# First twelve score-maximum fills moved into the last five blocks of the projection stage, with its PSUM banks and input buffers laid out anew

## The reference

```python
mod = (silu(c) @ wmod).reshape(2, 6, 1, -1)
sa, ca, ga, sb, cb, gb = (mod[:, 0], ..., mod[:, 5])   # ga, gb are kept at least 0.25 from zero
h = layernorm(x) * (1 + ca) + sa
x = x + ga * attention(h)       # 16 heads of 16, causal, qkv = h @ W_qkv.T + b_qkv, then @ W_out.T + b_out
h = layernorm(x) * (1 + cb) + sb
x = x + gb * ffn(h)             # 256 -> 1024 -> 256, relu, each layer with 3 routed low-rank experts
```

## Time and profile before

| | us |
|---|---|
| median of 3 runs | 1308.25 (1307.49 to 1309.97) |
| profiled execution | 1304.39 |
| its span | 1302.4 |
| TensorE busy in the span | 1218.0 (94%) |
| VectorE busy | 933.2 (72%) |
| ScalarE busy | 800.5 (61%) |
| GpSimd busy | 178.0 (14%) |

### The profile page before, as it was taken

The page is one execution under the profiler, slowest core; times in us unless marked ns, Lnnn a source line. Parts: engine busy times, 40 slices in busy tenths (PEclk is TensorE's granted clock), DMA queues, the critical chain, the costliest instruction groups (busy, mean ns, idle before and its releaser), DMA issues.

```text
span 1302.4 us, 24602 instructions
## 1 busy us (share of the span) xinstructions
PE 1218.0 (94%) x9928; PEld 723.5 (56%) x9928; DVE 933.2 (72%) x1247; ACT 800.5 (61%) x1611; POOL 178.0 (14%) x153
## 2 busy tenths in 40 slices
PE   6988789999999999999999999999998899999997
PEld 5875334444444444444444444444444788898886
DVE  5877897888787887778887778786631576766553
ACT  4451466777777776767777667777675554444442
POOL 5205600000211000000000000200110132222310
PEclk9987798999999999999999999999899999999999
DMA  5793120031032021013003003500000222111100
GB/s 170 247 289 144 52 64 10 8 87 34 27 108 70 10 65 54 3 45 98 10 13 90 19 10 93 138 10 10 3 10 27 50 65 65 53 38 50 57 17 33
DMA packets 58121, 79.58 MB, mean 61 GB/s; under 512 B 12680, under 2 KB 28752, under 8 KB 58008
## 3 DMA queue, kind: packets, MB, share of 16 engines
q1 hardware_dynamic: 58008, 78.01, 20.3%
HBM read 47.57 MB, written 29.62 MB: 59 GB/s over the span
## 4 chain that ended last, share of the span: by engine, by line
PE 67%; DVE 12%; ACT 9%; issue 8%; SPq 2%; DMA 1%; POOL 0%; POOLq 0%; ACTq 0%; DVEq 0%
PE ps L907 21%; PE ps L882 17%; PE ps L863 9%; PE ps L391 8%; ACT prob L1121 7%; PE ps L1008 5%; DVE mx L1270 5%; PE ps L820 4%; PE ps L811 2%; DVE xhat L419 1%; DVE hid_lo L1413 1%; SPq L453 1%; ACT o_sb L1106 1%; DVE stats L409 1%; DMA wqkv_sb<-in_wqkvT 1%
## 5 line engine op out<-in xcount | busy, mean ns | idle before, releaser
L1121 ACT ACTIVATE prob<-ps 128x512 f32<-128x512 f32 (+3 forms) x1280 | 598.1, 537 | 263.0 <-PE ps L820 161.3
L1270 DVE TENSOR_REDUCE mx<-ps 128x2 f32<-128x1024 f32 (+1 forms) x512 | 594.0, 1188 | 148.2 <-PE ps L863 85.5
L882 PE MATMUL ps<-qst,kst 64*128 64x512 f32 (+3 forms) x1280 | 387.0, 446 | 18.9 <-ACT prob L1121 14.3
L882 PEld LDWEIGHTS ps<-qst,kst 64*128 64x128 f32 x1280 | 183.9, 188 | 270.2 <-ACT prob L1121 211.3
L907 PE MATMUL ps<-prob,vw 128*32 128x512 f32 (+3 forms) x3032 | 317.8, 492 | 3.4 <-ACT o_sb L1106 3.4
L863 PE MATMUL ps<-kst,qst 62*128 62x512 f32 (+3 forms) x1280 | 288.7, 425 | 21.5 <-DVE mx L1270 18.1
L863 PEld LDWEIGHTS ps<-kst,qst 62*128 62x128 f32 x1280 | 137.1, 193 | 95.4 <-DVE mx L1270 51.5
L907 PEld LDWEIGHTS ps<-prob,vw 128*32 128x32 f32 x3032 | 60.5, 108 | 86.9 <-issue 38.7
L820 PE MATMUL ps<-mask_kh,eye_h 64*128 64x128 bf16 x1024 | 99.6, 225 | 0.0
L1266 DVE TENSOR_REDUCE mx<-ps 128x4 f32<-128x512 f32 x64 | 60.9, 955 | 30.8 <-PE ps L811 30.4
L1413 DVE TENSOR_TENSOR hid_lo<-hidf,hid_hi 128x512 fp32r<-128x512 f32 x64 | 68.0, 1095 | 20.7 <-ACT hid_hi L1161 20.6
(11 more groups left out here) (157 smaller groups left out, 1350.5 us busy)
## 6 DMA issues: line engine op xcount, KB each, us to landing
qk_parts<-parts SPq DMA_DIRECT2D x32, 512.0 KB, 5.4
qst<-qk_parts SPq DMA_DIRECT2D x192, 64.0 KB, 2.4
kst<-qk_parts SPq DMA_DIRECT2D x192, 64.0 KB, 2.4
xs<-in_x SPq DMA_DIRECT2D x16, 512.0 KB, 8.4
o_all<-o_sb SPq DMA_DIRECT2D x32, 256.0 KB
o_raw<-o_all SPq DMA_DIRECT2D x16, 256.0 KB
rd<-rden_rows SPq DMA_DIRECT2D x16, 256.0 KB
out<-y SPq DMA_DIRECT2D x8, 512.0 KB, 3.2
```

The costliest lines, as they stand in the source:

```text
L882: last = pe.matmul(ps[:, L_BANK + (4 * n + h) % L_BUFS, 0:BLK - skip], kst[g % 2][rows, h // 2, t * P:(t + 1) * P], qst[g % 2][rows, h // ...
L1121: act.activation(prob[:, n % P_BUFS, h, 0:width], ps[:, L_BANK + i % L_BUFS, 0:width], ACT.Exp).then_inc(exp_done, 1)
L1270: dve.tensor_reduce(mx[:, u % 2, :, pairs[0], r, cb], ps[:, bank:bank + 2, 0:width], AX, ALU.max).then_inc(max_red, 1)
```

## The change

- **Fills.** Twelve fills (`EARLY`) run inside the first stage: two in block 3, three in blocks 4 and 5, two in blocks 6 and 7. Unit 0's turn becomes fill 7, right behind the first fill of unit 1, with negative, high and low directly ahead of it on VectorE. `ORDER[0]` is now these twelve, `ORDER[1]` holds 14 fills, and from `ORDER[2]` on nothing differs.
- **Banks.** Transposes use bank 0 alone (a half waits for the other's modulation), v banks 1 and 2, q/k products a ring of three, banks 3 to 5, early fills banks 6 and 7 alone, each waiting for the maximum of the one before.
- **x.** Five input buffers; blocks 2 to 5 are loaded ahead of the loop and in its first iteration.
- **Order.** TensorE: first half of `turn(n+1)`, product 0, second half, product 1, all fills of the block but the last two, product 2, one fill, product 3, one fill, v. VectorE: the maxima stand in like manner between the `qk_low` of single tiles. In block 0 the second half of the first transposes follows the second `columns`.
- **SyncE.** `store_m(0)` is issued ahead of block 6's `store_parts`.

The `maxima`, `negative` and like functions are moved ahead in the file unchanged, apart from taking the bank from `bank_of(e)`. The core of the diff:

```diff
+X_BUFS = 5
@@ max_events
-            if i - lag in ends:
+            if ends.get(i - lag, 0) > 0:
                 events.append((kind, ends[i - lag]))
+        if ends.get(i - 1) == 0:
+            events += [(kind, 0) for kind in ("neg", "high", "low", "turn")]
@@
+EARLY_OF = {3: 2, 4: 3, 5: 3, 6: 2, 7: 2}
+EARLY = sum(EARLY_OF.values())
+EARLY_FROM = {n: sum(c for m, c in EARLY_OF.items() if m < n) for n in EARLY_OF}
@@ slots
-    done = TURN_FILL[0] + 1 + 4
+    done = EARLY
@@ build_program
-        T_BANK, V_BANK, QK_BANK, COL_BANK = 0, 2, 4, 7
-        S_BANK, L_BANK, L_BUFS, O_BANK = 0, 4, 3, 7
+        V_BANK, QK_BANK, QK_BUFS, COL_BANK = 1, 3, 3, 7
+        T_BANK, S_BANK, L_BANK, L_BUFS, O_BANK = 0, 0, 4, 3, 7
+        def bank_of(e):
+            return 6 if e < EARLY else S_BANK + 2 * (e % 2)
+        def qk_bank(n, c):
+            return QK_BANK + (n * 2 * KC + c) % QK_BUFS
@@ SyncE
                 def load_x(n):
-                    until(sp, xhat_done, n - 1)
-                    sp.dma_start(xs[:, n % 2], xb_in[n]).then_inc(x_in[n % 2], 16)
+                    until(sp, xhat_done, n - X_BUFS + 1)
+                    sp.dma_start(xs[:, n % X_BUFS], xb_in[n]).then_inc(x_in[n % X_BUFS], 16)
-                load_x(2)
+                for n in range(2, X_BUFS):
+                    load_x(n)
                 for n in range(NBLK):
-                    if n + 3 < NBLK:
-                        load_x(n + 3)
+                    if n + X_BUFS < NBLK:
+                        load_x(n + X_BUFS)
+                    if n == NBLK - 2:
+                        store_m(0)
                     store_parts(n)
@@ TensorE
+                def turn(n, k):
                     pe.wait_ge(xhat_done, n + 1)
-                    until(pe, h_out, n * 2 * KC)
+                    until(pe, h_out, (n * KC + k) * 2)
...
+                def project_qk(n, c):
                     pe.wait_ge(h_lo, n + 1)
-                        until(pe, qk_lo, (n - 1) * 2 * KC + c + 1)
+                    until(pe, qk_lo, n * 2 * KC + c - QK_BUFS + 1)
...
                 def fill(e):
-                    until(pe, max_red, e - 1)
+                    until(pe, max_red, e if e < EARLY else e - 1)
...
+                columns(((0, 1), (1, 0)), COL_BANK)
+                pe.wait_ge(consts, 4)
+                turn(0, 0)
+                columns(((2, 4), (3, 3)), COL_BANK - 1)
+                turn(0, 1)
+                pe.wait_ge(w_lo, 2)
+                project_qk(0, 0)
+                project_qk(0, 1)
+                turn(1, 0)
+                project_qk(0, 2)
+                turn(1, 1)
+                project_qk(0, 3)
+                pe.wait_ge(setup, 2 * KC)
+                gate_rows()
+                project_v(0)
+                for n in range(1, NBLK):
+                    es = [EARLY_FROM[n] + k for k in range(EARLY_OF[n])] if n in EARLY_OF else []
+                    if n + 1 < NBLK:
+                        turn(n + 1, 0)
+                    project_qk(n, 0)
+                    if n + 1 < NBLK:
+                        turn(n + 1, 1)
+                    project_qk(n, 1)
+                    for e in es[:-2]:
+                        fill(e)
+                    project_qk(n, 2)
+                    for e in es[-2:-1]:
+                        fill(e)
+                    project_qk(n, 3)
+                    for e in es[-1:]:
+                        fill(e)
+                    project_v(n)
@@ VectorE, in the loop over blocks, after moments, rescale and low
-                    qk_low(n)
+                    qk_low(n, 0)
+                    qk_low(n, 1)
+                    for e in es[:-2]:
+                        events(e)
+                    qk_low(n, 2)
+                    for e in es[-2:-1]:
+                        events(e)
+                    qk_low(n, 3)
+                    for e in es[-1:]:
+                        events(e)
                     v_rows(n)
```

More of the change, by code:

```diff
@@ L162 @@
 SLOT_OF = {e: s for s, es in enumerate(ORDER) for e in es}
-STORE_M = {u: SLOT_OF[TURN_FILL[u]] for u in range(NU)}
+STORE_M = {u: SLOT_OF[TURN_FILL[u]] for u in range(1, NU)}
 STORE_O = {u: min(NS, LAST[u] + PV_LAG + 2) for u in range(NU)}
@@ L1208, in modulations, with qk_low @@
                                           1.0 - v % 2, None, ALU.add).then_inc(mod_out, 1)
[L1210 to L1215, removed]
+                def qk_low(n, c):
+                    dve.wait_ge(qk_hi, n * 2 * KC + c + 1)
+                    dve.scalar_tensor_tensor(out=parts[:, n % 2, 1, c, :], in0=ps[:, qk_bank(n, c), :],
+                                             scalar=bq_sb[:, c:c + 1], in1=parts[:, n % 2, 0, c, :].bitcast(F32),
+                                             op0=ALU.add, op1=ALU.subtract).then_inc(qk_lo, 1)
                 def v_rows(n):
@@ new lines, in invert, with low_o @@
+                def invert(g):
+                    for q in range(2):
+                        dve.wait_ge(o_stored[q], 16 * O_DMAS * NJ // 2 * (g + 1))
+                    until(dve, rden_stored[g % 2], 16 * (g // 2))
+                    dve.reciprocal(rden[:, g % 2, :], den[:, g % 2, :]).then_inc(rden_done, 1)
+                link = Links(dve, dve3)
+                def low_o(i):
+                    dve.wait_ge(o_hi, i + 1)
+                    dve.tensor_tensor(oT[1][:], o_raw[:, i % 2], oT[0][:].bitcast(F32), ALU.subtract).then_inc(o_lo, 1)
@@ new lines, in gated, with add_x @@
+                def gated(i, bank):
+                    q, b = i % 2, BLOCKS[i] // NJ
+                    return dve.tensor_tensor(x1[:, q], ps[:, bank:bank + 2, :].rearrange("p a (t d) -> p (a t) d", t=2),
+                                             gates[:, 0, b:b + 1, :].broadcast_to((P, TT, D)), ALU.mult)
+                def add_x(i):
+                    q = i % 2
+                    dve.wait_ge(xbias_done, i + 1)
+                    dve.tensor_tensor(x1[:, q], x1[:, q], xs2[:, q], ALU.add).then_inc(x1_done, 1)
+                    dve.wait_ge(x1_done, i + 1)
+                    statistics(dve, link, x1[:, q], stats2, mv2, var2)
@@ new lines, in front_modulate @@
+                def front_modulate(e):
+                    b = BLOCKS[0] // NJ
+                    dve.wait_ge(fill_done, e + 1)
+                    for k in range(KC):
+                        last = dve.tensor_scalar(hf2[:, k, :], ps[:, bank_of(e) + k, :],
+                                                 mod[:, b, 2, k:k + 1], mod[:, b, 3, k:k + 1], ALU.mult, ALU.add)
+                        if k < KC - 1:
+                            link(last, wait=False)
+                    last.then_inc(max_red, 1)
@@ new lines, in event @@
+                def event(i, ev):
+                    if ev[0] == "max":
+                        maxima(FILL_OF[i], ev)
+                    if ev[0] == "neg":
+                        negative(ev[1])
+                    if ev[0] == "high":
+                        m_high_part(ev[1])
+                    if ev[0] == "low":
+                        m_low_part(ev[1])
+                    if ev[0] == "turn":
+                        copy_turned(FILL_OF[i], ev[1])
+                    if ev[0] == "project":
+                        front_residual(FILL_OF[i])
+                    if ev[0] == "rescale":
+                        standardise_x1(0)
+                    if ev[0] == "turn_x":
+                        front_modulate(FILL_OF[i])
@@ L1223, in _, with events @@
+                def events(e):
+                    for i in range(FILLS[e - 1] + 1 if e > 0 else 0, FILLS[e] + 1):
+                        event(i, EVENTS[i])
                 dve.wait_ge(exp_c, 1)
@@ L1339, in front_modulate @@
-                def front_modulate(e):
-                    b = BLOCKS[0] // NJ
-                    dve.wait_ge(fill_done, e + 1)
-                    for k in range(KC):
-                        last = dve.tensor_scalar(hf2[:, k, :], ps[:, S_BANK + 2 * (e % 2) + k, :],
-                                                 mod[:, b, 2, k:k + 1], mod[:, b, 3, k:k + 1], ALU.mult, ALU.add)
-                        if k < KC - 1:
-                            link(last, wait=False)
-                    last.then_inc(max_red, 1)
@@ L1349, in _ @@
-                done = 0
-                for i, ev in enumerate(EVENTS):
-                    if ev[0] == "max":
-                        while INVERT[done] < SLOT_OF[FILL_OF[i]] - 1:
-                            invert(done)
-                            done += 1
-                        maxima(FILL_OF[i], ev)
-                    if ev[0] == "neg":
-                        negative(ev[1])
-                    if ev[0] == "high":
-                        m_high_part(ev[1])
-                    if ev[0] == "low":
-                        m_low_part(ev[1])
-                    if ev[0] == "turn":
-                        copy_turned(FILL_OF[i], ev[1])
-                    if ev[0] == "project":
-                        front_residual(FILL_OF[i])
```

(14 more changed lines are left out.)

187 lines of the change are left out of this document (73 added, 114 removed).

## The result

| | before | changed |
|---|---|---|
| median, us | 1307.87 (1306.21 to 1309.97, 4 runs) | 1332.35 (1329.35 to 1336.51, 4 runs) |
| profiled execution, us | 1304.39 | 1333.6 |
| its span, us | 1302.4 | 1331.7 |

The ratio is 1.0193, 95% interval 1.0172 to 1.0214. The forecast was 1330, slower.

The account below looks back on a forecast made before the run. It took TensorE, with three input waits, to bound the first stage, then VectorE's maxima; +11.0 + 5.3 + 13.0 - 12.3 = +17.0, +5.6 for the clock, made +22.6: about 1330 us, range 1318 to 1341.

Parts of the forecast that it names:

- The ring's wait and the two engines taking turns: First stage: each block's fourth q/k product waits for the first's low part on VectorE; TensorE stands 2.4 us.
- Block 0: First block: late first product and a wait before the fourth; block 1 starts at 45.9 instead of 34.90, +11.0 us.
- Blocks 1 and 2: First-stage blocks without fills: 12.0 us each, 2.7 more than before, together +5.3 us.
- Blocks 3 to 7: First-stage blocks with early fills: stalls at fills 3, 6 and the turn; 67.7 us against 54.7, +13.0.
- The clock: TensorE's pauses in the first stage: one fall in block 0, one more later, 2.8 us a fall, together +5.6.
- the third rival: First stage: the clock falls in every pausing block, +34 us, 1342; 20 in 100.
- Fill 12 after V: Start of attention: VectorE starts fill 12 2.9 us after the last V product instead of 15.2, saving 12.3 us.
- The sum: Whole kernel: +17.0 us at full clock, +5.6 for the clock, +22.6 in all; median about 1330.
- the shift reaches the end one for one: After step 0 the order of fills is unchanged, so a shift there was taken to reach the end in full.
- The faster rival: Fourth q/k product finds its bank free, blocks 1 and 2 stay at 9.34 us; about 1298; 8 in 100.

Follow-up runs that it names:

- late4: late3 with the q/k products going round a ring of four banks instead of three; 1304.19 us, ratio 0.9966.
- order: Changed kernel, only VectorE's and ScalarE's order altered: product 0's low part ahead of low(n+1) and standardising, its high part between modulations; 1306.91 us, ratio 1.0005.
- busy3: late3 with unread matmuls ahead of each block's fourth product, 8 a block and 32 in block 0; 1330.02 us, ratio 1.0179.
- after2: The changed kernel, unaltered, measured and profiled a second time; 1331.78 us, ratio 1.0192.
- late3: Changed kernel with the twelve early fills moved behind the first stage, in two pairs of banks, ring of three kept; 1336.59 us, ratio 1.0231.
- x5: The kernel before with five input buffers and nothing else; 1299.87 us, ratio 0.9953.
- b0: Changed kernel with one product, the fourth of block 0, put into the free bank 6; 1329.68 us, ratio 1.0179.
- tailb: x5b with unit 0's six fills inside blocks 6 and 7, in the transposes' first bank pair; 1300.11 us, ratio 0.9943.
- x5b: x5 with the 24 stack loads of blocks 2 and 3 issued behind the last stored parts; 1299.12 us, ratio 0.9934.

## Why the prediction was right, point by point

- **The ring's wait and the two engines taking turns.** Right, in mechanism and size. The low part of product 0 ends at 7.7 us into a block by the working; the fourth product started 8.09 us after the block's start in blocks 1 and 2 (56.58 - 48.49). late4 gives the ring its fourth bank back and the loss goes. order leaves it and takes away what stood ahead of the low part, and the loss goes too: the cause is the two together, as the step put it.
- **Block 0.** 20.4 expected for the first product, 20.86 found; 36.75 for the fourth, 36.50; 45.9 for block 1 at full clock, 48.49 found. The fall was counted, and at its 2.8 us it would be 48.7.
- **Blocks 1 and 2** at 12.0: 12.42 in the block without a fall, and 12.4 in busy3. 0.4 us of handoffs a block were missing.
- **Blocks 3 to 7.** 13.4, 14.8, 17.2, 11.8, 10.5 expected; 14.8, 16.6, 19.1, 12.1, 10.4 found. The stalls stand where they were put (fills 3 and 6, the turn). The sum was 67.7 and is 73.0; of the 5.3 that are missing 5.1 are in blocks 3 to 5, where the clock fell; three falls at busy3's price would be 4.65 (an estimate), the rest handoffs.
- **The clock was the mis-sized term.** I took two falls at 2.8 us. There were more, cheaper ones: of the five blocks with a pause only block 1 had none in the first profile and all five had one in the second (after2), as in late3. In after2 block 0 ends 1.3 us earlier instead (47.19 against 48.49), so how often and how long the clock is low differs between executions of one kernel. Price by busy3: 1.55 us. A fall here lasted about 3.3 us (an estimate: PEclk 0.88 over 13.94 us), where the row of before had 6.2 us at the lower level. Over block 0 and blocks 2 to 5 the excess over my full-clock times is 9.6 us, where I had 5.6; some 0.4 us a block of it are the handoffs. The rule of the Trainium skill ("TensorE: Matmul & The Clock Gate", section "A second HAM failure mode: psum-queue depth-cycling"), that short pauses between groups swing the clock, described this better than my weighing of it: a fall in every pausing block, as the third rival had it, though not at its price.
- **Fill 12 after V.** 2.9 us expected, 2.6 found.
- **The sum, and luck in it.** The shift at fill 12 is 26.9 us against 22.6: block 0 gave 13.6 (11.0 and a fall of 2.8 expected), blocks 1 and 2 7.7 (5.3), blocks 3 to 7 18.3 (13.0), and 12.7 were saved behind V (12.3). That the shift reaches the end one for one held within 4 us: 27.1 at unit 4, 23.2 at unit 29, 29.3 at the end of the span. The medians are 24.5 apart, less than the profiled executions (29.2), since those lie on opposite sides of their medians; that brought 1330 closer than the terms deserve, and is luck.
- **The faster rival** was 6 to 9 us too low even where the ring's wait is gone: 1304 with the fills behind the stage (late4), 1307 with them in it (order), against its 1298. x5 alone comes to 1299.9 and holds none of the early fills: what gain there was came from the waits for x.

## What to carry to other kernels

Before a ring of buffers is made shorter, look up what stands ahead of the instruction that frees a slot, on its own engine, and what that in turn waits for: where the chain comes back to the waiting engine within one iteration, the two engines take turns, and one slot more (late4), or a few instructions moved (order), is worth more than the work that was to be hidden. Try each part of such a change by itself; here one part alone, five input buffers, gave 0.5%, and no version with early fills was faster than the same one without them by more than its interval. In these kernels a pause of 2.4 us on TensorE mostly cost more than its length: behind nine of ten such pauses (late3, b0 and the two profiles of the changed kernel) a stretch at half clock followed.

## What the runs showed that I had not expected

- In late3 the pause ahead of the fourth product was followed by the lower clock in every one of five blocks (PEclk 0.88 over the block), and matmuls that do nothing, put into the pause, kept it at 1.00 and made the kernel some 6 us faster.
- With the x waits gone the stores of parts were next: with 24 DMAs of 64 KB between them ScalarE waited 9 us, and moving the 24 behind the stores ended the wait. That is worth a look at the order of issues, though the runs don't tell SyncE's issuing time from the DMA engines' load.
- Fills hidden in the stage cost nearly what they save. Six brought the last fill of the twelve 0.4 us ahead (tailb against x5b) and no time. Twelve, with the ring's wait gone, cost 15.6 us in blocks 3 to 7 (63.0 in order, 47.4 in late4) and gave 14.0 back (fill 12 2.6 us after the last V, against 16.6); the two kernels differ in ring and order too, so this is an estimate.
